# Interaction network on one core: two groups of layer 3 split in all four tiles

## What is computed

```python
x = x0
for (W, b), split in zip(conv_params, split_flags):      # flags True, True, False
    h = x.shape[1]
    z = jnp.einsum('bhd,bmd->bhmd', x, x0).reshape(B, h * x0.shape[1], D)
    xk = jax.nn.relu(jnp.einsum('oc,bcd->bod', W, z) + b[None, :, None])
    if split:
        half = xk.shape[1] // 2
        x, xk = (xk[:, :half], xk[:, half:])
    else:
        x = xk
    results.append(xk)
pooled = jnp.sum(jnp.concatenate(results, axis=1), axis=2)
return pooled @ Wo.T + bo
```

## Time and profile before

| | |
|---|---|
| median of 3 runs | 476.99 us (476.26 to 477.19) |
| profiled execution, its own time | 476.04 us |
| its span, first to last instruction | 474.3 us |
| busy: TensorE, VectorE, GpSimd, ScalarE | 94%, 90%, 86%, 66% |
| 128x1536 subtraction on GpSimd, 128x1024 | 3.52 us, 2.42 us |
| 128x1536 product on VectorE, 128x512 | 1.75 us, 0.68 us |
| 128x512 subtraction on VectorE (L594) | 0.68 us |
| last group's low matmuls end | 470.12 us |

### The profile page before, as it was taken

How to read it: one execution, slowest core, us unless ns; L and a number is a source line. 1 busy time by engine, 2 the same in 40 slices (tenths; PEclk the granted TensorE clock), 3 DMA queues, 4 the chain that set the end, 5 groups by cost and what they waited for, 6 DMA issues and landing times.

```text
span 474.3 us, 5975 instructions
## 1 busy us (share of the span) xinstructions
PE 443.5 (94%) x1601; PEld 302.2 (64%) x1601; DVE 425.9 (90%) x489; ACT 310.8 (66%) x383; POOL 408.4 (86%) x147
## 2 busy tenths in 40 slices
PE   0758499999999999999999999999999999999997
PEld 0325365676767767676766767666766767677774
DVE  1557599999999999999999999999999999999997
ACT  1224667685868767585868767685877768577661
POOL 0107399998999999999999999999999999899995
PEclk9988799999999999999999999999999999999999
DMA  8999999979595959879595968969495963922100
GB/s 211 242 234 228 248 229 211 224 171 228 117 228 119 224 121 215 172 162 214 124 230 110 222 133 193 205 138 238 103 229 119 225 144 69 198 44 46 25 19 1
DMA packets 23232, 78.42 MB, mean 165 GB/s; under 512 B 5939, under 2 KB 5939, under 8 KB 18996
## 3 DMA queue, kind: packets, MB, share of 16 engines
q1 hardware_dynamic: 23220, 78.28, 75.3%
HBM read 61.48 MB, written 0.00 MB: 130 GB/s over the span
## 4 chain that ended last, share of the span: by engine, by line
PE 84%; DMA 6%; DVE 4%; SPq 2%; ACT 1%; issue 1%; POOL 1%; DVEq 0%
PE y_ps L694 26%; PE y_ps L700 15%; PE y_ps L682 15%; PE y_ps L684 15%; PE y_ps L690 7%; PE y_ps L706 4%; DMA a_rep<-x_sb 3%; DVE z L530 3%; DMA w_raw<-w_dram 2%; DMA shifted<-xt_dram 1%; PE y_ps L660 1%; POOL zl L481 1%; SPq L329 1%; PE y_ps L686 1%; PE y_ps L702 1%
## 5 line engine op out<-in xcount | busy, mean ns | idle before, releaser
L481 POOL TENSOR_TENSOR zl<-z,zh 128x1024 fp32r<-128x1024 f32 (+1 forms) x141 | 406.6, 2920 | 48.6 <-ACT zh L423 48.3
L530 DVE TENSOR_TENSOR z<-a_ps,b_fac 128x1536 f32<-128x1536 f32 x254 | 269.7, 1083 | 24.4 <-PE y_ps L706 12.0
L423 ACT ACTIVATE zh<-z 128x1024 fp32r<-128x1024 f32 (+1 forms) x141 | 176.8, 1254 | 111.9 <-DVE z L530 111.5
L700 PE MATMUL y_ps<-zl,w_high 128*128 128x512 f32 x332 | 154.0, 557 | 2.3 <-POOL zl L481 2.3
L682 PE MATMUL y_ps<-zh,w_high 128*128 128x512 f32 x332 | 131.8, 397 | 8.4 <-ACT zh L423 8.4
L684 PE MATMUL y_ps<-zh,w_low 128*128 128x512 f32 x332 | 130.8, 394 | 0.0
L694 PE MATMUL y_ps<-z,w_raw 128*128 128x512 f32 x254 | 129.9, 593 | 0.0
L700 PEld LDWEIGHTS y_ps<-zl,w_high 128*128 128x128 f32 x332 | 62.2, 188 | 71.0 <-issue 61.1
L682 PEld LDWEIGHTS y_ps<-zh,w_high 128*128 128x128 f32 x332 | 62.7, 189 | 23.7 <-issue 6.4
L684 PEld LDWEIGHTS y_ps<-zh,w_low 128*128 128x128 f32 x332 | 63.0, 190 | 13.8
L694 PEld LDWEIGHTS y_ps<-z,w_raw 128*128 128x128 f32 x254 | 48.0, 189 | 10.6
(11 more groups left out here) (45 smaller groups left out, 166.9 us busy)
## 6 DMA issues: line engine op xcount, KB each, us to landing
b_fac<-xt_dram SPq DMA_DIRECT2D x60, 512.0 KB, 8.9
shifted<-xt_dram SPq DMA_DIRECT2D x64, 256.0 KB, 4.9
a_rep<-x_sb SPq DMA_DIRECT2D x96, 128.0 KB, 3.1
shifted<-xt_dram SPq DMA_DIRECT2D x64, 128.0 KB, 5.2
a_rep<-x_sb SPq DMA_DIRECT2D x64, 64.0 KB, 2.6
b_fac<-xt_dram SPq DMA_DIRECT2D x8, 256.0 KB, 10.6
w_raw<-w_dram SPq DMA_DIRECT2D x2, 640.0 KB, 13.0
w_raw<-w_dram SPq DMA_DIRECT2D x2, 384.0 KB, 12.3
```

Source lines behind the costliest of these rows:

```text
L423: nc.scalar.activation(zh[:, slot, 0:end - native, :], z[:, slot, native:end, :], ACT.Copy).then_inc(zh_ready, 1)
L481: nc.gpsimd.tensor_tensor(zl[:, slot, 0:end - native, :], z[:, slot, native:end, :], zh[:, slot, 0:end - native, :].bitcast(F32), ALU.subtract
L530: return nc.vector.tensor_tensor(dst, factor.unsqueeze(1).to_broadcast(list(dst.shape)), others, ALU.mult)
L700: mm = nc.tensor.matmul(y, wh[layer][:, w, :], zl[:, slot, t, :], start=False, stop=end_here)
```

## The change

In layer 3, groups 1 and 3 (positions 6 and 8) have no native tile any more. Their first three tiles go to GpSimd, the fourth goes the way of VectorE's tile: product into PSUM, rounding by ScalarE, subtraction by VectorE. The subtraction of position 6 stands behind P7; that of position 8 is carried into the next iteration, behind its P0 (`carried`), and in iteration 17 it stands ahead of `early_samples`. The PSUM banks are dealt out anew. The fourth tile's high and low parts lie in two new buffers, whose memory is that of w1_sb, the staging of layer 1's weights; terms and out_sb lie in a2_rep and x1_sb. Where a wait counted native products, it counts those left (`natives_before`) or VectorE's tiles.

```diff
-SPLIT = {1: (2,), 2: (3, 3, 3, 3), 3: (3, 3, 3, 3)}
-BY_DVE = {1: (1,), 2: (1, 0, 1, 0), 3: (1, 0, 1, 0)}
-ZX_BANK = {0: 1, 1: 0, 3: 1, 5: 0, 7: 1}
+SPLIT = {1: (2,), 2: (3, 3, 3, 3), 3: (3, 4, 3, 4)}
+BY_DVE = {1: (1,), 2: (1, 0, 1, 0), 3: (1, 1, 1, 1)}
+ZX_BANK = {0: 0, 1: 1, 3: 0, 5: 0, 6: 1, 7: 0, 8: 1}
+FOURTH = {6: 0, 8: 1}
 X_TILE = {1: 2, 2: 3, 3: 3}
-POOL_TILE = {1: 3, 2: 1, 3: 1}
+POOL_TILE = {1: (3,), 2: (1, 1, 1, 1), 3: (1, 0, 1, 0)}
...
+def natives_before(i):
+
+    if isinstance(i, int) and (i < 2 or i > NCHUNK):
+        return sum(not lacks_native(layer, g) for k in range(i) for layer in layers_of(k) for g in range(GROUPS[layer]))
+    per_iter = sum(not lacks_native(layer, g) for layer in GROUPS for g in range(GROUPS[layer]))
+    return i * per_iter + (natives_before(1) + sum(not lacks_native(layer, g) for layer in layers_of(1)
+                                                   for g in range(GROUPS[layer])) - 2 * per_iter)
+
+
+def lacks_native(layer, g):
+
+    return SPLIT[layer][g] == GT
...
-        w1_sb = sb("w1_sb", [P, 2 * GT + 2, P])
...
-        terms = sb("terms", [P, EARLY])
+        terms = a_rep[2][:, 0, 0:EARLY]
         ones = sb("ones", [P, 1])
-        out_sb = sb("out_sb", [1, BATCH])
+        out_sb = x_out[1][0:1, :]
+
+        early = ExitStack()
+        w1_sb = early.enter_context(nc.sbuf_tensor("w1_sb", [P, 2 * GT + 2, P], F32))
+        wq_raw = w1_sb[:, 2 * GT:, :]
+        early.close()
+        fourth = {"high": sb("zh_fourth", [P, 2 * CH], F32R), "low": sb("zl_fourth", [P, 2 * CH], F32R)}
+
+        def dve_part(kind, pos, slot, part):
+
+            if pos in FOURTH:
+                return fourth[kind][:, FOURTH[pos] * CH:(FOURTH[pos] + 1) * CH]
+            return {"high": zh, "low": zl}[kind][:, slot, part, :]
...
-                    sp.wait_ge(z_native_ready, groups_before(c))
+                    sp.wait_ge(zx_ready, dve_tiles_before(c))
...
-                        act.wait_ge(z_native_ready, groups_before(i))
+                        act.wait_ge(z_native_ready, natives_before(i))
+                        act.wait_ge(zx_ready, dve_tiles_before(i))
...
-                pool = POOL_TILE[layer] if by_dve else native
+                pool = POOL_TILE[layer][g] if by_dve else native
                 multiply(z[:, slot, native:end, :], factor, others[:, pool:pool + end - native, :]).then_inc(z_ready, 1)
                 if by_dve:
-                    done = e - 1 if pos == 1 else e
+                    done = e - 1 if pos in (6, 7, 8) or pos == 1 and exists(i) or pos == 0 and carried(i) else e
...
-                multiply(z[:, slot, 0:native, :], factor, others[:, 0:native, :]).then_inc(z_native_ready, 1)
+                if native:
+                    multiply(z[:, slot, 0:native, :], factor, others[:, 0:native, :]).then_inc(z_native_ready, 1)
...
+            def carried(i):
+
+                return not isinstance(i, int) or 2 < i <= NCHUNK + 1
...
                     if pos - 1 in here and pos - 1 in ZX_BANK and not is_native(here[pos - 1][0][3]):
                         subtract(i, *here[pos - 1])
+                    if pos == 0 and carried(i):
+                        last = steps(i - 1)[-1]
+                        subtract(i - 1, last, len(steps(i - 1)) - 1)
...
                     if pos == 8 and i_is(i, NCHUNK + 1):
+                        subtract(i, *here[8])
                         early_samples()
...
-                    pe.wait_ge(z_native_ready, q + 1)
+                    if native:
+                        pe.wait_ge(z_native_ready, n + 1)
```

More of the change, by code:

```diff
@@ L150, in steps @@
 def steps(i):
-    found, q, e = [], groups_before(i), dve_tiles_before(i)
+    found, q, e, n = [], groups_before(i), dve_tiles_before(i), natives_before(i)
     for layer, g, by_dve in dve_tiles(i):
-        found.append((FIRST[layer] + g, layer, g, q + len(found), e))
+        found.append((FIRST[layer] + g, layer, g, q + len(found), e, n))
         e = e + by_dve
+        n = n + (not lacks_native(layer, g))
     return found
@@ L201, in cin_kernel @@
         wl = {layer: sb(f"w{layer}_low", [P, spl[layer], P], F32R) for layer in (1, 2, 3)}
-        wq_raw = w1_sb[:, 2 * GT:, :]
         wq = sb("wq", [P, 2, P], F32R)
@@ L366, in _ @@
             sp.wait_ge(out_ready, 2)
-            sp.dma_start(out.rearrange("b o -> o b"), out_sb[:]).then_inc(out_stored, 16)
+            sp.dma_start(out.rearrange("b o -> o b"), out_sb).then_inc(out_stored, 16)
             sp.wait_ge(out_stored, 16)
@@ L417, in body @@
                     if pos in here and not is_native(here[pos][0][3]):
-                        (pos, layer, g, q, e), k = here[pos]
+                        (pos, layer, g, q, e, n), k = here[pos]
                         slot, (native, end, by_dve) = slot_of(i, k), parts_of(layer, g)
@@ L426, in body @@
                             act.wait_ge(zx_ready, e + 1)
-                            nc.scalar.activation(zh[:, slot, end - native, :], zx_ps[:, ZX_BANK[pos], :], ACT.Copy
+                            nc.scalar.activation(dve_part("high", pos, slot, end - native), zx_ps[:, ZX_BANK[pos], :], ACT.Copy
                                                  ).then_inc(zxh_ready, 1)
@@ L475, in body @@
             def body(i):
-                for k, (pos, layer, g, q, e) in enumerate(steps(i)):
+                for k, (pos, layer, g, q, e, n) in enumerate(steps(i)):
                     if is_native(q):
@@ L514, in early_samples @@
                 dve.wait_ge(pooled3_done, NCHUNK - 1)
-                nc.vector.tensor_scalar(terms[:], pooled3[:, 0:EARLY], cols_sb[:, 4:5], None, ALU.mult
+                nc.vector.tensor_scalar(terms, pooled3[:, 0:EARLY], cols_sb[:, 4:5], None, ALU.mult
                                         ).then_inc(terms_made, 1)
@@ L533, in product @@
             def product(i, step, k):
-                pos, layer, g, q, e = step
+                pos, layer, g, q, e, n = step
                 c, slot, (native, end, by_dve) = i - (layer - 1), slot_of(i, k), parts_of(layer, g)
@@ L586, in product @@
                              ).then_inc(zx_ready, 1)
-                multiply(z[:, slot, 0:native, :], factor, others[:, 0:native, :]).then_inc(z_native_ready, 1)
+                if native:
+                    multiply(z[:, slot, 0:native, :], factor, others[:, 0:native, :]).then_inc(z_native_ready, 1)
             def subtract(i, step, k):
-                pos, layer, g, q, e = step
+                pos, layer, g, q, e, n = step
                 slot, (native, end, by_dve) = slot_of(i, k), parts_of(layer, g)
                 dve.wait_ge(zxh_ready, e + 1)
-                nc.vector.tensor_tensor(zl[:, slot, end - native, :], zx_ps[:, ZX_BANK[pos], :],
-                                        zh[:, slot, end - native, :].bitcast(F32), ALU.subtract
+                nc.vector.tensor_tensor(dve_part("low", pos, slot, end - native), zx_ps[:, ZX_BANK[pos], :],
+                                        dve_part("high", pos, slot, end - native).bitcast(F32), ALU.subtract
                                         ).then_inc(zxl_ready, 1)
+            def carried(i):
+                return not isinstance(i, int) or 2 < i <= NCHUNK + 1
             def body(i):
@@ L689, in body @@
                         for weights in (wh, wl):
-                            nc.tensor.matmul(y, weights[layer][:, x_weights, :], zh[:, slot, x_part, :],
+                            nc.tensor.matmul(y, weights[layer][:, x_weights, :], dve_part("high", pos, slot, x_part),
                                              start=False, stop=False)
-                    pe.wait_ge(z_native_ready, q + 1)
+                    if native:
+                        pe.wait_ge(z_native_ready, n + 1)
                     for t in range(native):
@@ L705, in body @@
                         pe.wait_ge(zxl_ready, e + 1)
-                        mm = nc.tensor.matmul(y, wh[layer][:, x_weights, :], zl[:, slot, x_part, :],
+                        mm = nc.tensor.matmul(y, wh[layer][:, x_weights, :], dve_part("low", pos, slot, x_part),
                                               start=False, stop=last)
@@ L716, in _ @@
             pe.wait_ge(terms_made, 3)
-            nc.tensor.matmul(y_ps[1][0:1, 0:EARLY], ones[:], terms[:], start=True, stop=True).then_inc(out_summed, 1)
+            nc.tensor.matmul(y_ps[1][0:1, 0:EARLY], ones[:], terms, start=True, stop=True).then_inc(out_summed, 1)
             pe.wait_ge(last_begun, 1)
```

## The result

The changed kernel takes 480.52 us (median of 6 runs, 479.96 to 482.37) against 476.97 us (6 runs): ratio 1.0084, 95% interval 1.0069 to 1.0099. It is slower, by 3.55 us where 5.8 were forecast: under 1%, but clear of the noise. The profiled execution's span is 478.4 us, 4.1 more than before.

What follows compares the result with a forecast made beforehand. TensorE set the pace before; after the change a loop through VectorE, ScalarE, GpSimd and TensorE would bound. Start +1.7, steady periods +0.2, end +3.9 sum to +5.8 us: 482.8 us, range 476.8 to 485.7.

Steps and rivals of the forecast that it cites:

- TensorE saves 0.17 a group: Groups 6 and 8 on TensorE: a native tile (0.86) gives way to three float32r matmuls (0.69), 5.5 us in all.
- VectorE's own work, 26.7: Steady iteration: VectorE's work without waits rises from 25.5 to 26.7 us through two added subtractions of 0.60.
- The round, 26.95 (26.85 to 27.12): Steady loop through VectorE, ScalarE, GpSimd, TensorE: 26.29 us plus 0.83 at most; period taken as 26.95, +0.2 over 12 periods.
- the short release of P0: VectorE's product for group 0 would start 0.20 us, not 0.39, after TensorE frees its slot.
- the 0.08 of overlap: Overlap between VectorE instructions, lost at its wait before the product for group 0, may come back: 0.08 us.
- The rule on the pipe: Skill's rule that VectorE's next operation waits for an empty pipe: 0.68 per subtraction, 1.0 us more; forecast used 0.60.
- The start, +1.7: Before the steady iterations: two new VectorE subtractions 1.2 us, longer weight splits 0.5; ends 1.5 and 2.0.
- The end, +3.9: Iterations 15 to 17 on VectorE: six subtractions 3.6 us, three ScalarE waits 3.0, less 2.7 of old waits.
- VectorE alone bounds: Rival, chance 0.15: loop hand-overs shorten, VectorE's 26.70 us sets the period; 479.8 us.
- TensorE keeps the pace: Rival, chance 0.11: added subtractions fall into VectorE's waits, TensorE gains all 5.5 us, the end pays 3.9; 475.4 us.
- A wait on ScalarE inside the loop: Rival, chance 0.08: an added ScalarE rounding delays the loop by 0.4, period 27.4 us; 488.2 us.
- The cancellation: Rival, chance 0.08: loop at 26.7 us and an end that pays only 1; about 477 us.

Runs made afterwards that it cites:

- experiment 1: Changed kernel with pool12 moved on VectorE from ahead of to behind the product for group 2: 476.09 us, ratio 0.9984 to the kernel before.
- the fifth experiment: Changed kernel with pool12 behind VectorE's product for group 2 and VectorE's low part ahead of GpSimd's in groups 6 and 8: 475.83 us, ratio 0.9987.
- the seventh experiment: Kernel before with only group 8 (by position) split in all four tiles, group 6 left as it was: 479.59 us, ratio 1.0063.
- the second: Changed kernel with VectorE's low-part matmul taken ahead of GpSimd's three in groups 6 and 8: 478.26 us, ratio 1.0021 to the kernel before.
- The third and fourth: Kernel before plus a useless 1.13 us VectorE reduction, at the product for group 1 (third) or group 3 (fourth): 483.81 and 479.11 us.
- the eighth and ninth runs: The change in iterations 3 to 15 only, with pool12 behind VectorE's product for group 2 (eighth) or not moved (ninth): 473.72 and 478.48 us.

## Why the prediction was right, and where it was off

**TensorE saves 0.17 a group: right, and not gained.** Group 8 took 2.77 where nothing held it (experiment 1). In the changed kernel the saving went into waits for GpSimd.

**VectorE's own work, 26.7: right within 0.1.** The rows of the changed kernel give 26.6, and the fifth experiment 26.59 without a wait.

**The round, 26.95 (26.85 to 27.12): right, the value for another reason.** Measured 26.98 on average and 27.02 piece by piece. The prediction came down from 27.12 to 26.95 by the short release of P0, 0.20; it was 0.38, the long one. What shortened the sum was the other item, the 0.08 of overlap: from P0 to P2 it is 6.98, not 6.45 + 0.60 = 7.05, and GpSimd's run of groups 2 to 6 is 15.22, not 15.26. Its two additions were shown one by one: 0.60 between P0 and P2 by the move of pool12 (and, with the rest left open there, by the seventh experiment), the fourth matmul behind GpSimd by the second. The third and fourth show the same round in the kernel before, where nothing of the change is present.

**The rule on the pipe.** The rows say 0.60 from the carried subtraction (245.05) to P1 (245.65) and from 248.57 to 249.16, with durations of 0.68. The Trainium skill, VectorE: DVE Perf Modes, section The DRAIN you can't avoid, says that the next operation doesn't start until the pipe is empty, but adds that one which isn't held starts earlier. The prediction weighed the first half only; the trace agrees with the second for these instructions, and the 1.0 more that the first would have cost did not come.

**The start, +1.7: 1.53.** The two subtractions cost 1.19, as forecast (1.2). The longer splits cost 0.27 where 0.5 was taken, and 0.07 is scatter from before. They took 2.28 and 2.60 against 2.29 and 2.46: most of such a duration is the wait for GpSimd's running subtraction (0.95 alone), and the wait does not grow by a sixth with the columns.

**The end, +3.9: the term that was mis-sized, 2.0 measured.** The three waits for ScalarE came as said, each 0.84 shown, and the sum's start came 3.48 later against P2 of iteration 15 (470.10 - 410.92 = 59.18, before 464.53 - 408.83 = 55.70). What failed is that the prediction added only what stands ahead of the sum and carried the sum itself over at its old length, without a reason. Its steps took 5.45 before (464.53 to 469.98), since they stood still beside GpSimd's last two subtractions; now they begin while only the last one is left, and take 4.30. A further 0.3 went behind it, against the prediction's sentence that the rest behind the sum is unchanged: before, the end hung on TensorE's last matmul (470.12) and ScalarE's evacuation, and the sum was ready first; now it hangs on the sum. TensorE's own end is close behind: the last pool3 still waited 0.17 for the evacuation. The 2.0 lies under the 2.6 that this term had as its lower end; that the total stayed inside the range is owed to the width of the other terms.

**The rivals.** That VectorE alone bounds was 0.3 an iteration too low: the loop through GpSimd stood in front of it, and taking 0.60 out of the loop brought it to that bound. That TensorE keeps the pace is refuted. A wait on ScalarE inside the loop did not come; VectorE waited for it in the last three subtractions of group 8 only. The cancellation did not come either: the round stayed at 26.98, and the end paid 2.0.

## What to carry to other kernels

When several engines are near full, the shares don't say which one bounds. Follow a buffer's slot round through all engines and add it up: what is inserted is paid where it lies on that round, and free beside it, so the same instruction can cost much or nothing by its place in an engine's order (here 0.34 of 0.60 an iteration, and 0.43 of 1.13 against nothing). Start and end of a software pipeline have other waits than its middle; a trade that pays in the middle can be switched off there. A duration in a trace can hold a wait: before it is carried over to a changed kernel, see what ran beside it.

## What the runs showed of the hardware

VectorE's instructions with two inputs in SBUF (the weight splits, the last two steps of the sum) and the sum's first step, with one, do not run beside GpSimd's subtraction. The first step, begun at 470.10, ended at 472.83, 0.26 after GpSimd's instruction, and the same one took 0.45 when it fell between two of them. In the eighth and ninth runs it began with two of GpSimd's subtractions, back to back, still to finish, and took 4.73 and 4.72. It holds the other way too: in the kernel before, GpSimd's 128x1024 subtraction at 62.84 met the split begun at 61.41 and took 3.12, where others took 2.42. The trace counts the wait as duration, for either engine.

VectorE's products and subtractions, with one input in PSUM, kept 1.75 and 0.68 beside a busy GpSimd, and its sums over the dimension, with one input in SBUF, 0.68.
